# A five-sweep graph kernel: the second layer's weights applied before its sweeps, neighbour counts in four column quarters, one weight eviction per chunk on VectorE, a join in two parts

## The reference

```python
h = relu(layernorm(x)); x = x + 1.0 - 0.1 * h - 0.01 * sum(h * (adj @ h), axis=1)      # layer 0
h = relu(layernorm(x))                                                              # layer 1, two hops
for k in range(2):
    h = tanh(concatenate([adj @ h, h], axis=1) @ W[k])
x = x + h
h = relu(layernorm(x)); x = x + w @ (h @ weight) + bias                                # layer 2
# w: per row of adj the last 100 nonzero entries, weighted 1, 1/2, 1/4, ... from the last one back
h = relu(layernorm(x))                                                              # layer 3
x = x + tanh([h, t] @ W1 + b1) @ W2 + b2 + adj @ (h @ B.T) - rowsum(adj) * (h @ B.T)
```

## Time and profile before

| | us |
|---|---|
| median of 3 runs | 762.15 (760.29 to 762.63) |
| the profiled execution | 756.76 |
| its span, first to last instruction | 755.0 |
| L0, blocks of TensorE | 12.6 to 184.0 |
| L1A | 184.0 to 316.9 |
| L1B | 316.9 to 458.3 |
| L2 | 458.3 to about 617 |
| L3 | to 755 |

### The profile page before, as it was taken

One profiled execution on the slowest core, in us unless ns is written; L12 is line 12 of the kernel. 1 busy time (PEld: TensorE's weight loads), 2 busy tenths in 40 slices (PEclk: granted clock), 3 DMA queues, 4 the chain that ended last, 5 costly groups with the idle time before them and its releaser, 6 DMA issues. The chain is left out here.

```text
span 755.0 us, 10045 instructions
## 1 busy us (share of the span) xinstructions
PE 699.3 (93%) x3642; PEld 279.3 (37%) x3656; DVE 446.5 (59%) x765; ACT 183.1 (24%) x271; POOL 103.2 (14%) x126
## 2 busy tenths in 40 slices
PE   1899899998989999999999997999899989999997
PEld 0333333333333333444444443444344433333332
DVE  5766676777888878846665556688788740000000
ACT  2010111100100000101111113888788832000010
POOL 5011011111100000001222222011111121211210
PEclk9899999999999999999999999999999999999999
DMA  9999999996699999699998986699999839999994
GB/s 369 374 366 415 415 420 414 413 412 242 250 395 408 329 374 388 260 375 377 364 372 317 368 319 217 244 405 337 341 366 370 302 128 348 372 407 410 364 398 167
DMA packets 49680, 262.58 MB, mean 348 GB/s; under 512 B 6880, under 2 KB 18912, under 8 KB 19296
## 3 DMA queue, kind: packets, MB, share of 16 engines
q1 hardware_dynamic: 39136, 252.51, 85.8%
q10 hardware_dynamic: 10496, 9.44, 4.0%
HBM read 255.76 MB, written 6.16 MB: 347 GB/s over the span
## 5 line engine op out<-in xcount | busy, mean ns | idle before, releaser
L1144 PE MATMUL accA<-land,X 128*64 128x512 f32 x1504 | 363.0, 600 | 8.6 <-DMA land<-adj_blocks 7.7
L1144 PEld LDWEIGHTS accA<-land,X 128*64 128x64 f32 x1504 | 100.9, 137 | 183.8 <-issue 140.9
L1144 PE MATMUL accA<-cache,X 128*64 128x512 f32 x544 | 133.3, 601 | 17.4 <-DVE X L1009 12.6
L958 DVE TENSOR_TENSOR uS<-uS,land 128x512 f32<-128x512 f32 x186 | 130.6, 702 | 30.5 <-DMA land<-adj_blocks 20.9
L976 DVE TENSOR_SCALAR uS<-land 128x1024 bf16<-128x1024 f32 (+1 forms) x188 | 125.8, 720 | 38.0 <-DMA land<-adj_blocks 37.1
L481 ACT ACTIVATE wS<-spare 128x1024 uint16<-128x1024 f32 x112 | 108.2, 1033 | 31.1 <-PE spare L1176 30.4
L1176 PE MATMUL spare<-uS,triA 128*128 128x512 bf16 x247 | 74.8, 382 | 15.5 <-DVE wS L479 11.4
L638 POOL TENSOR_TENSOR hS<-tS 128x256 f32<-128x256 f32 x24 | 21.2, 883 | 425.7 <-DVE tS L839 425.7
L942 DVE TENSOR_TENSOR tS<-uS,nat 128x256 f32<-128x256 f32 x8 | 3.4, 422 | 122.9 <-PE nat L1076 122.9
L1187 PE MATMUL accA<-wS,X 128*128 128x512 bf16 x251 | 75.4, 381 | 0.4
L1144 PEld LDWEIGHTS accA<-cache,X 128*64 128x64 f32 x544 | 38.7, 138 | 91.0 <-issue 83.3
(11 more groups left out here) (83 smaller groups left out, 388.2 us busy)
## 6 DMA issues: line engine op xcount, KB each, us to landing
land<-adj_blocks SPq DMA_DIRECT2D x219, 1024.0 KB, 7.1
...
uS<-counts SPq DMA_DIRECT2D x64, 4.0 KB
...
```

The lines of the kernel that those rows point to most:

```text
L958: nc.vector.tensor_tensor(total, total, of[:, i * W:(i + 1) * W], ALU.add)\
L1144: last = nc.tensor.matmul(accA[k * D:(k + 1) * D, c % 2, :], tile(X[p % 2], TQ * q + k), of[:, k * W:(k + 1) * W], start=(b == 0), stop=(b ...
```

## The change

Three things are changed.

**The hops.** The layer-1 products are turned round: instead of (adj @ h) @ Wa + h @ Wb the kernel computes adj @ (h @ Wa) + h @ Wb, and h @ [Wa Wb] is made ahead, chunk by chunk, at the end of the sweep before. For that L0 and L1A get a transpose of the chunk's rows (`turn`, L1092 in the changed kernel), an ACT copy (`turned`), four f32 products of 64 rows x 128 x 128 (`hop`, L1151) into `spare`, and two ACT evictions (`hopped`, L771) to X and to Z. Z lies in `wS`, which L2's evictions write later, so those wait for it. In L1A and L1B the transposes of own rows, `wx` and `wagg` go; four transposes of `accS` (as in L3) take their place, DVE adds Z and the two halves (`hop_added`, L897 and L898), and ACT takes the tanh from SBUF. The row sums' result moves from the bank of `nat` to that of `tr`.

**The counting.** The two matmuls of a block's count now have 32 weight columns each, in a quarter of TensorE's columns given by the tile number modulo 4; an ACT copy and one matmul (`stack`, L1157) add the four quarters up. Counts and left weights have 32 rows instead of 64. The table puts the last of these DVE steps (`left`, L954) at block 10 of the next chunk.

**L2.** Of 16 evictions one (block 6) is on DVE, in order, instead of two, one block late. The join is done in two halves, after blocks 3 and 4.

```diff
-EVAC_DVE = (4, 12)
-EVAC_LAG = 1
+EVAC_DVE = (6,)
+EVAC_LAG = 0
...
+STAGES_L0 = {0: 1, 1: 2, "part": 3, 3: 5, "stack": 5, "counts": 6, 4: 7, 5: 8, "weights": 8, 6: 10, "left": 10, 7: 11,
+             "left out": 12, "turn": 13, "turned": 13, "hop": 14, "hopped": 15}
...
+JOINS_L2 = {3: "join0", 4: "join1"}
...
-        upperS = wS[0:D, :].bitcast(F32)[:, 0:W]
-        countS = wS[0:D, :].bitcast(BF16)[:, 2 * W:3 * W]
-        loadjS = wS[0:D, :].bitcast(F32)[:, 2 * W:3 * W]
-        lolaterS = wS[0:D, :].bitcast(BF16)[:, 3 * W:4 * W]
-        loweightS = wS[0:D, :].bitcast(U16)[:, 6 * W:7 * W]
+        Z = wS[:, :].bitcast(F32)
+        loS = later[0:NT, :].bitcast(F16)
+        loadjS = lowS[:, :].bitcast(F32)
+        partS = rowsT[:, :].bitcast(BF16)
+        lomostS = partS[0:NT, :].bitcast(U16)
+        loweightS = countS[NT:2 * NT, :].bitcast(U16)
...
-        sums_p = nat[:, CH:CH + 4]
+        sums_p = tr[:, CH:CH + 4]
...
+            else:
+                eng.wait_ge(nat_evac, nat_no(L1B, 2 * n + 1) + 1)
...
-                if at == 0 and p in (L1A, L1B):
-
-                    act.wait_ge(tr_done, tr_no(p, c, 0) + 1)
-                    if nat_no(p, c):
-                        act.wait_ge(nat_done, nat_no(p, c))
-                    rows_transposed()
...
+                    if p in (L0, L2):
+                        act.wait_ge(nat_done, nat_no(p, c, 0) + 1)
                         if copied_no(p, c):
                             act.wait_ge(copy_used, copied_no(p, c))
-                        nc.scalar.activation(natS[:, :], nat[:, 0:CH],
-                                             ACT.Tanh if p == L1B else ACT.Copy).then_inc(nat_evac, 1)
+                        nc.scalar.activation(natS[:, :], nat[:, 0:CH], ACT.Copy).then_inc(nat_evac, 1)
+                if at == "tanh":
+                    act.wait_ge(nat_evac, nat_no(p, c, 0) + 1)
+                    if p == L1B:
+                        act.wait_ge(copy_used, copied_no(p, c))
+                    nc.scalar.activation((hS if p == L1A else natS)[:, :], tS[:, :], ACT.Tanh).then_inc(tanh_done, 1)
+                if at == "hopped":
+                    act.wait_ge(hop_done, hop_no(p, c) + 1)
+                    for of, to in ((0, X[1] if p == L0 else X[0]), (1, Z)):
+                        nc.scalar.activation(chunk(to, ch(p, c)).rearrange("p (b t d) -> p b t d", b=2, d=D),
+                                             hop_out(of), ACT.Copy).then_inc(hop_evac, 1)
...
+                    if p in (L0, L1A):
+                        act.wait_ge(left_made, min(c + 1, NC - 1) if p == L0 else NC)
...
+                if at == "part":
                     act.wait_ge(counted, NQ * (c + 1))
                     if c:
-                        act.wait_ge(count_ready, c)
-                    nc.scalar.activation(upperS, spare[D:P, c % 2, :], ACT.Copy).then_inc(count_half, 1)
-                if p == L0 and at == 7:
+                        act.wait_ge(left_made, c)
+                        act.wait_ge(hop_done, hop_no(L0, c - 1) + 1)
+                    if c == NC - 1:
+                        act.wait_ge(hop_done, hop_no(L0, c) + 1)
+                    nc.scalar.activation(partS[:, :], spare[:, c % 2, :], ACT.Copy).then_inc(parts_out, 1)
+                if at == "weights":
                     act.wait_ge(count_ready, c + 1)
-                    act.dma_start(counts_d[c], countS).then_inc(counts_out, 16)
-                    act.wait_ge(left_later, c + 1)
-                    if c:
-                        act.wait_ge(left_out, 16 * c)
-                    nc.scalar.activation(loweightS, lolaterS, ACT.Relu, bias=wt("full", rows=(0, D)),
-                                         scale=-BIT * BIT).then_inc(left_made, 1)
+                    act.dma_start(counts_d[c], countS[0:NT, :]).then_inc(counts_out, 16)
...
+                def hop_added():
...
+                    dve.wait_ge(nat_done, nat_no(p, c, 0) + 1)
+                    dve.wait_ge(hop_evac, 2 * hop_no(p - 1, ch(p - 1, ch(p, c))) + 2)
+                    parts = nat[:, :].rearrange("p (t h d) -> p h t d", h=2, d=D)
+                    L(nc.vector.tensor_tensor(rows4(tS), rows4(chunk(Z, ch(p, c))), parts[:, 0], ALU.add))
+                    nc.vector.tensor_tensor(rows4(tS), rows4(tS), parts[:, 1], ALU.add).then_inc(nat_evac, 1)
...
-                        norm_rows(p, c, chunk(X[1], c))
-                        dve.wait_ge(count_half, c + 1)
+                        norm_rows(p, c, hS[:, :])
+                    if at == "counts":
+                        dve.wait_ge(stacked, c + 1)
                         if c:
                             dve.wait_ge(counts_out, 16 * c)
-                        nc.vector.tensor_tensor(countS, upperS, spare[0:D, c % 2, :], ALU.add).then_inc(count_ready, 1)
+                            dve.wait_ge(left_most, c)
+                        nc.vector.tensor_copy(countS[0:NT, :], spare[0:NT, c % 2, :]).then_inc(count_ready, 1)
...
+                    if at == "left":
                         dve.wait_ge(left_adj, 16 * (c + 1))
...
+                        dve.wait_ge(left_most, c + 1)
                         if c:
-                            dve.wait_ge(left_made, c)
-                        nc.vector.scalar_tensor_tensor(out=lolaterS, in0=loadjS, scalar=0.0, in1=countS,
-                                                       op0=ALU.is_equal, op1=ALU.max).then_inc(left_later, 1)
+                            dve.wait_ge(left_out, 16 * c)
+                        nc.vector.scalar_tensor_tensor(out=loweightS, in0=loadjS, scalar=0.0, in1=lomostS,
+                                                       op0=ALU.not_equal, op1=ALU.mult).then_inc(left_made, 1)
...
+                    if at == "added":
+                        dve.wait_ge(sums_done, c + 1)
+                        nc.vector.tensor_scalar(rowsum[:, c * 4:(c + 1) * 4], sums_p, -1.0, None, ALU.mult)\
+                            .then_inc(rowsum_ready, 1)
+                        hop_added()
...
-                if at == 0 and p in (L1A, L1B):
-
-                    tr_free(tr_no(p, c, 0))
-                    transposed(lambda j: tile(X[p % 2], 4 * ch(p, c) + j))
...
+                if p == L2 and at in ("join0", "join1") or p == L2 and c == NC - 1 and at == 1:
+                    parts = {"join0": (0, 1), "join1": (2, 3)}.get(at, (0, 1, 2, 3))
+                    if at != "join1":
+                        nat_free(nat_no(p, c, 0))
+                        pe.wait_ge(acc_evac, NC * p + c + 1)
+                    for j in parts:
+                        last = nc.tensor.matmul(nat[:, j * D:(j + 1) * D], accS[:, j * P:(j + 1) * P],
+                                                wt("join"), start=True, stop=True)
+                    if at != "join0":
+                        last.then_inc(nat_done, 1)
...
+                        tr_free(tr_no(p, c))
...
-                    if p in (L1A, L1B):
-                        pe.wait_ge(tr_evac, tr_no(p, c, 0) + 1)
-                        k = 0 if p == L1A else 1
-                        for j in range(2):
-                            nc.tensor.matmul(nat_pair(j), rows_t(j), wt(f"wx{k}"), start=(j == 0), stop=False)
...
-                    if p in (L1A, L1B):
-                        for j in range(4):
-                            last = nc.tensor.matmul(nat[:, j * D:(j + 1) * D], accS[:, j * P:(j + 1) * P],
-                                                    wt(f"wagg{k}"), start=False, stop=(j == 3))
...
+                    for j in range(4):
+                        if p in (L1A, L1B, L3):
                             last = nc.tensor.transpose(nat[:, j * P:(j + 1) * P], accS[:, j * P:(j + 1) * P],
                                                        wt("ident"))
...
+                    tr_free(tr_no(p, c))
+                    if p == L1A:
+                        pe.wait_ge(tanh_done, tanh_no(p, c) + 1)
+                    else:
+                        pe.wait_ge(h_ready, row_no(p, c) + 1)
...
+                if at == "hop":
+
+                    pe.wait_ge(tr_evac, tr_no(p, c) + 1)
+                    if hop_no(p, c):
+                        pe.wait_ge(hop_evac, 2 * hop_no(p, c))
+                    for t in (0, 2, 1, 3):
+                        half = (t // 2 * D, t // 2 * D + D)
+                        last = nc.tensor.matmul(spare[:, 2 + t // 2, t % 2 * P:(t % 2 + 1) * P],
+                                                rows_t(t % 2)[half[0]:half[1], :],
+                                                wt("hop0" if p == L0 else "hop1", rows=half), start=True, stop=True)
+                    last.then_inc(hop_done, 1)
+                if at == "stack":
+                    pe.wait_ge(parts_out, c + 1)
+                    nc.tensor.matmul(spare[0:NT, c % 2, :], later[:, 2 * NT:3 * NT], partS[:, :],
+                                     start=True, stop=True).then_inc(stacked, 1)
...
-                elif p == L1A:
```

(19 more changed lines are left out.)

107 lines of the change are left out of this document (56 added, 51 removed).

## The result

The changed kernel takes 772.9 us (median of 4 runs, 771.8 to 779.0) beside 761.9 us of the kernel before on the same chip: ratio 1.017, 95% interval 1.013 to 1.021. Its profiled execution took 771.83 us, span 769.9. The change is slower, by 1.7%, where 1.5% was forecast.

The account below looks back on a forecast made before the run. Transfers bind L0 before the change, TensorE after it. 756.76 + 24.9 (L0) + 0.5 (L1A) - 7.8 (L1B) - 6.2 (L2) = 768.2 us, times 1.0071 = 773.6 us; range 750 to 784, 765 to 787 by its own terms' bounds.

Parts of the forecast that it names:

- The deciding term: L0: each switch between 64-wide sweep and 32-wide counts and back costs 0.24 us, 16 a chunk; L0 +24.9 us.
- The hop: L0, per chunk on TensorE: 0.64 us of products with 0.10 before and 0.05 behind, 0.79 us.
- `left` at nothing, or 3.5 us once: DVE's wait for a late transfer in L0: nothing if TensorE binds, 3.5 us once at L0's end if transfers bind.
- The first rival: L0: 32-wide counts cost no shape change, transfers stay the bound; 750.8 us (743 to 757), chance 0.22.
- L2's first chunk: Start of L2: TensorE's 3.58 us wait for DVE shrinks, -1.2 us.
- the chance of faster: Whole run: chance 0.29 of faster than before by more than 2.3 us; slower 0.62, within 0.09.
- L1A, +0.5 forecast: L1A: TensorE's work per chunk 2.05 against 1.95 us, counted as nothing; first chunk's late rows +0.5 us (-1 to +7).
- The next chunk waited for transfers anyway: L1A's first chunk: the last rows' transpose at block 9 comes before its rows; costed at only +0.5 us.
- The fourth rival: L1A: VectorE becomes the bound, 0.9 us more in seven chunks, +6.3; 780 us with the forecast, chance 0.06.
- L1B, -7.8 forecast: L1B: TensorE saves 1.32 us a chunk, 10.6 in eight, less a 0.4 us wait in seven; -7.8 us (-10.6 to -5).
- L2, -6.2 forecast: L2: eviction wait goes, later layernorm costs 0.9; -0.7 us in seven chunks, first chunk -1.2; -6.2 us (-13 to 0).
- the second rival: L0: only the 0.10 us gap ahead of the counts costs; L0 +6.6 us, 755 us in all, chance 0.07.

Follow-up runs that it names:

- e1_wide: The changed kernel with the counts 64 weight columns wide again, in two column halves; 765.5 us, ratio 1.005 to the kernel before.
- e2_before_q: The kernel before with only the counts made 32 columns wide in four quarters; one execution took 776.3 us.
- e5_adj: e1_wide with the small transfer that `left` waits for issued behind the chunk's fourth transfer instead of the last; 755.0 us, ratio 0.997.
- e7_c0: e6_turn with DVE's eviction at block 12 instead of 6 in L2's first chunk only; 747.4 us, ratio 0.987.
- e6_turn: e5_adj with the steps of L1A's first chunk later, `turn` at block 12 instead of 9; 757.3 us, ratio 0.998.
- e4_l2_before: The changed kernel with only its L2 part undone (two late DVE evictions, join in one piece); 775.9 us, ratio 1.020 to the kernel before.

## Why the prediction was right, and where it was not

**The deciding term.** The round trip of the count's shape, 0.24 us taken from three gaps of other pairs of shapes, measured 0.255. With it came the chunk of 23.66 us, L0's end (207.9, forecast 208.9) and the turn of the bound from transfers to TensorE. e1_wide and e2_before_q show that it is this term: taken out of the changed kernel and put alone into the old one, it moves the pitch by 0.25 to 0.26 us each time. That the chunk came out to 0.02 us is in part luck. The hop was priced at 0.79 us, with a change of shape of its own, and takes 0.64, since beside the 32-wide count the shape changes anyway; the 16 round trips took 0.24 us more than forecast.

**`left` at nothing, or 3.5 us once.** As forecast it cost nothing in the changed kernel, with TensorE as the bound. The other branch was wrong: the step "it costs 3.5 us once, at the end of L0" took chunk 7's issue at 171.77 for a special case. The same issue stands at the end of every chunk's list, so the wait comes in every chunk: 13.1 us of VectorE, 8.2 us of L0. The trace of the kernel before had it to see: from the second to the seventh, each of these small transfers landed 9.6 to 13.7 us after its issue. The first rival was priced at 750.8 us for what measured 765.5. `left` is only a part of that: e5_adj, without the wait, still has the ratio 0.997, which is 760 us on the forecast's scale (762.15 x 0.997). e7_c0, which moves the eviction in L2's first chunk as well, comes to 0.987 or 752. So the second term that the rival had wrong is L2's first chunk, -1.2 us in the forecast: in e6_turn it takes 27.3 us beside 25.6 in the kernel before. In truth the change as built is not faster than before even without the round trip (ratio 1.005), and the chance of faster, 0.29, was too high for these two reasons.

**L1A, +0.5 forecast, +2.1 measured.** That the chunk's work stays the same was right: chunks without waits take 15.70 us beside 15.80. "The next chunk waited for transfers anyway" was too kind to the first chunk. TensorE waits 2.78 us at `turn` for the normed rows, and then the clock falls (granted clock 0.70 over 221 to 226 us):

```profile
220.69 1.12 PE L1092 MATMUL tr<-wts,hS 128*64 128x128 f32 x8 [2.78 <-DVE hS L886]
221.57 1.95 PE L1207 MATMUL accA<-land,X 128*64 128x512 f32 x4
223.45 0.95 PE L1151 MATMUL spare<-wts,rowsT 64*128 64x128 f32 x8
```

The sweep block from 221.57 to 223.45 takes 1.88 us instead of 0.86 to 0.96. The fourth rival, VectorE as L1A's bound, is refuted by the chunks of 15.70 us.

**L1B, -7.8 forecast, -6.1 measured.** The saving per chunk was right: chunks without waits take 16.89 us instead of 17.92, 1.03 less, made of the 1.32 forecast and of 0.25 of waiting at `turn` (forecast 0.4):

```profile
422.83 1.03 PE L1207 MATMUL accA<-land,X 128*64 128x512 f32 x4
423.94 0.66 PE L1092 MATMUL tr<-wts,hS 128*64 128x128 f32 x8
```

The block at 422.83 needs 0.86 and ends at 423.69. Eight times 1.03 is 8.2; some 2.5 us of it went to transfers, in seven waits of 0.23 to 0.52 us for `land`, where L1B's trace had none before. The faster TensorE catches up with the next bound; that term was missing.

**L2, -6.2 forecast, -4.9 measured.** The waits for DVE's eviction went and 0.2 to 0.7 us for `hS` came (forecast 0.9). First to last `accS`: -4.3 for seven chunks (forecast -5.0). That nearness is luck too: the other traces with the same order there give -0.6 to -3.8. The first chunk gave 1.4 (forecast 1.2); but e4_l2_before and e7_c0 show that the place of the eviction cost 1.5 there which could have been had.

**The sum.** The profiled execution was forecast at 768.2 and took 771.8: each stage behind L0 came out 1.3 to 1.7 us above its term, L0 1.1 below. Multiplying by 1.0071 then lifted the forecast to 773.6, while the changed kernel's median is only 1.001 of its profiled execution. So the nearness of 773.6 to 772.9 is in part luck: two errors of 4 us of opposite sign. Small slips in the prediction's own sums don't matter here: at 0.20 us a round trip its terms give +19.8 for L0 and not +19.6, at 0.30 +32.5 and not +32.7, and the second rival's +6.6 should be +7.1.
